# Splitting the stored rows into seven batches and the last, and starting the expert layer inside the last batch's attention

## The reference

```python
def reference(x, ctx, mask, ...):
    x = x + mamba_block(layernorm(x))            # own layernorm, conv, scan in chunks, gated norm, residual
    x = x + cross_attention(layernorm(x), ctx, ctx, adj, mask, Wq, bq, Wk, bk, Wv, bv, Wo, bo)
    x = x + expert_layer(layernorm(x))
    return x

def expert_layer(x):                             # x: batch, position, feature
    scores = positional_encoding(512, 32) @ sign(tile_sigs).T
    expert = argmax(scores, axis=-1)             # one of 8 for each of the 512 positions, the same in all batches
    return W[expert] @ x + b[expert]
```

## Time and profile before

| | us |
|---|---|
| median of 3 runs | 1262.71 |
| lowest, highest | 1261.99, 1266.43 |
| the profiled execution | 1266.53 |
| its span, first to last instruction | 1264.7 |
| granted TensorE clock, mean over the span | 0.969 of full speed |
| TensorE busy over the span | 1135.1 (90%) |
| DVE, ACT, POOL busy | 1005.2, 781.2, 634.1 |

### The profile page before, as it was taken

One profiled execution on the slowest core, in us unless ns is written; L12 is line 12 of the kernel. 1 busy time (PEld: TensorE's weight loads), 2 busy tenths in 40 slices (PEclk: granted clock), 3 DMA queues, 4 the chain that ended last, 5 costly groups with the idle time before them and its releaser, 6 DMA issues. The chain is left out here.

```text
span 1264.7 us, 29914 instructions
## 1 busy us (share of the span) xinstructions
PE 1135.1 (90%) x10292; PEld 840.7 (66%) x10292; DVE 1005.2 (79%) x2535; ACT 781.2 (62%) x1452; POOL 634.1 (50%) x554
## 2 busy tenths in 40 slices
PE   4687999999999999999999999999999999877397
PEld 2355677777777676867777777777776777755244
DVE  6866888888879887888888887888888877754486
ACT  2224676667666676667766766676566776766242
POOL 4572466337732684357544763278245753300475
PEclk9798999999999999999999999999899999989699
DMA  6042105400522024301440054104230133110511
GB/s 207 0 117 76 51 7 141 122 26 26 145 74 76 27 76 108 111 5 59 114 139 5 26 151 112 33 26 120 65 117 10 61 77 103 28 49 15 208 80 57
DMA packets 101524, 96.52 MB, mean 76 GB/s; under 512 B 17184, under 2 KB 76832, under 8 KB 100096
## 3 DMA queue, kind: packets, MB, share of 16 engines
q1 hardware_dynamic: 92912, 76.42, 20.4%
q0 software_dynamic: 6240, 17.57, 5.9%
q10 hardware_dynamic: 2224, 0.62, 0.2%
HBM read 71.49 MB, written 27.26 MB: 78 GB/s over the span
## 5 line engine op out<-in xcount | busy, mean ns | idle before, releaser
L907 ACT ACTIVATE T<-T,nmx 128x512 f32<-128x512 f32 x512 | 369.2, 724 | 214.7 <-DVE nmx L1278 211.8
L1278 DVE CUSTOM_DVE_ANT_0 T<-ps,am 128x512 f32<-128x512 f32 x512 | 348.0, 685 | 108.8 <-PE ps L501 106.6
L697 PE MATMUL pt<-ident,T 128*128 128x128 f32 x2048 | 314.1, 276 | 15.5 <-ACT PT L898 14.1
L697 PEld LDWEIGHTS pt<-ident,T 128*128 128x128 f32 x2048 | 250.0, 142 | 93.6 <-issue 42.3
L501 PE MATMUL ps<-k_st,q_st 128*128 128x512 f32 x512 | 261.5, 512 | 24.8 <-DMA q_st<-q_d 24.8
L898 ACT COPY PT<-pt 128x512 f32<-128x512 f32 x352 | 201.7, 573 | 16.4 <-PE pt L697 16.2
L1394 POOL TENSOR_TENSOR dmask<-triu,dA 128x1024 fp32r<-128x1024 f32 x64 | 132.7, 2137 | 49.5 <-DVE dA L1122 49.4
L716 PE MATMUL po<-PT,va 128*17 128x128 f32 x4096 | 137.6, 275 | 13.4 <-issue 7.0
L501 PEld LDWEIGHTS ps<-k_st,q_st 128*128 128x128 f32 x512 | 98.9, 193 | 55.1 <-DMA q_st<-q_d 28.0
L716 PEld LDWEIGHTS po<-PT,va 128*17 128x17 f32 x4096 | 102.4, 97 | 36.8 <-issue 35.4
L1369 POOL TENSOR_TENSOR xc<-xc,ygT 128x512 f32<-128x512 f32 x90 | 119.9, 1332 | 13.4
(11 more groups left out here) (218 smaller groups left out, 1968.3 us busy)
## 6 DMA issues: line engine op xcount, KB each, us to landing
k_st<-k_d SPq DMA_DIRECT2D x256, 64.0 KB, 2.2
q_st<-q_d SPq DMA_DIRECT2D x256, 64.0 KB, 2.4
am<-in_mask SPq DMA_DIRECT2D x8, 1024.0 KB, 5.4
k_d<-kp SPq DMA_DIRECT2D x32, 256.0 KB, 2.6
am<-in_adj POOLq DMA_DIRECT2D x8, 1024.0 KB, 10.8
q_d<-qp SPq DMA_DIRECT2D x128, 64.0 KB, 1.6
xio<-in_x SPq DMA_DIRECT2D x8, 512.0 KB, 4.3
xio<-in_ctxT SPq DMA_DIRECT2D x8, 512.0 KB, 4.1
```

What stands on the lines that cost most here:

```text
L697: ins = pe.transpose(pt[u % 2][:, kt * P:(kt + 1) * P], T[:, u % RING, kt * P:(kt + 1) * P], ident[:, :])
L907: act.activation(T[:, u % RING, :], T[:, u % RING, :], ACT.Exp, bias=nmx[:, u % RING:u % RING + 1], scale=-1.0).then_inc(sems["probs"], 1)
L1278: dve.tensor_tensor_reduce(T[:, u % RING, :], ps[(a * UNITS + u) % S_BANKS][:, :], ams[a % 2][:, qt, :], -1.0, 3e38, ALU.add, ALU.min, nmx ...
```

## The change

The tensor x2_d becomes two: x2_early holds the rows of batches 0 to 6 (7 KB a position), x2_late those of batch 7 (1 KB). Each block is gathered twice, from the one and from the other. New stages of the last batch only put expert work into its attention: "fb" the gathers of the biases, "fg" those of blocks 0 to 3 from x2_early (both on POOL), "fw" the load of the expert weights (SP), "fs" the statistics of blocks 0 to 2 for seven batches, two rows a slot in twelve consecutive slots (DVE), "fr" their powers (POOL), "fl" the placing of the weights of blocks 0 and 1 (ACT, eight copies). For that the tiles are laid out anew: the weights lie over wxbc, wz and pre (one tile proj), the biases over xt, xdt and xw (x3), the placed weights over am_0, am_1, th with sq and zs (tsz), and T, and the six blocks' rows have a buffer each.

The pairs are put in another order (PAIR): first the three pairs of batches 0 to 5 of blocks 0 to 3, twelve in all, then the pairs of batches 6 and 7 of these blocks, then blocks 4 and 5. They start within the slots: pair i stands in slot F_AT + 3 i on TensorE, a slot earlier on DVE (normalise) and a slot later on ACT (copy_pair), for the first five; the rest follow in loops. In a slot the pair stands behind the stages, so pair 0 follows the last group of weighted sums. POOL, in its loop of pairs, issues the gathers of blocks 4 and 5 at pairs 3 and 4, the six late gathers at pairs 6 to 8, the powers of the remaining groups of rows after pairs 3, 10, 14 and 18, and the scatters at pairs 14 to 17 and 21 and at the end. The third and fourth tiles' "ot" and "op" of the last batch get places of their own (FINAL).

```diff
+LAST = B - 1
+AHEAD = 4
+PAIR = [(k, n) for k in range(AHEAD) for n in range(B // 2 - 1)] + [(k, B // 2 - 1) for k in range(AHEAD)] + [(k, n) for k in range(AHEAD, BLOCKS) for n in range(B // 2)]
+ROWS = [[(k, j) for j in range(B - 1)] for k in range(AHEAD)] + [[(k, B - 1) for k in range(AHEAD)]] + [[(k, j) for j in range(B)] for k in range(AHEAD, BLOCKS)]
+SUMMED = [max(i for i, (kk, n) in enumerate(PAIR) if kk == k) + 1 for k in range(BLOCKS)]
+STATS_IN = 3
+PLACED_IN = 2
+PLACE_AT = (0, 4, 14, 16)
+STATS_AT = [(g, (2 * n, 2 * n + 1)) for g in range(STATS_IN, AHEAD) for n in range(B // 2)] + [(None, None)] * 6 + [(AHEAD, range(AHEAD))] + [
+    (g, (2 * n, 2 * n + 1)) for g in range(AHEAD + 1, BLOCKS + 1) for n in range(B // 2)]
...
+STAGES.update({("fw",): {"sp": 880}, ("fb",): {"pool": 600}})
+STAGES.update({("fg", k): {"pool": tick} for k, tick in enumerate((700, 820, 740, 780))})
+STAGES.update({("fs", k, n): {"dve": 980 + 80 * k + 20 * n} for k in range(STATS_IN) for n in range(B // 2)})
+STAGES.update({("fr", k): {"pool": 1045 + 80 * k} for k in range(STATS_IN)})
+STAGES.update({("fl", k, j): {"act": (1000, 1120)[k] + 20 * j} for k in range(PLACED_IN) for j in range(P // SEG)})
+FINAL = {
+    ("ot", 2): {"pe": 1080, "act": 1100}, ("op", 2): {"pe": 1140, "dve": 1150, "sp": 1160},
+    ("ot", 3): {"pe": 1400, "act": 1400}, ("op", 3): {"pe": 1420, "dve": 1420, "sp": 1440},
+}
...
+F_AT = SLOTS - 13
+F_PACE = 3
+def pairs_at(s_, ahead):
+    i, r = divmod(s_ - F_AT + ahead, F_PACE)
+    return [i] * (r == 0 and 0 <= i < PAIRS)
...
-        x2_d = nc.dram_tensor("x2_d", (S, ROW), F32, kind="Internal").ap()
+        x2_early = nc.dram_tensor("x2_early", (S, LAST * E), F32, kind="Internal").ap()
+        x2_late = nc.dram_tensor("x2_late", (S, E), F32, kind="Internal").ap()
...
+                    if k == "fw":
+                        last = latest([("bc", i) for i in range(CT)] + [("z", c) for c in range(C)], b)
+                        sp.wait_ge(full(last, b), full_at(last, b))
...
+                        sp.dma_start(w_f, t["w_f"].rearrange("(k p) t e -> p k t e", p=P)).then_inc(step["f_w"], 16)
...
+                def pair(i):
+                    pe.wait_ge(step["f_normed"], 2 * (i + 1))
+                    pe.wait_ge(step["f_copied"], max(0, i - 1))
+                    if i < 2:
+                        pe.wait_ge(sems[evac_by(UNITS - 2 + i)], at(evac_by(UNITS - 2 + i), LAST, evac_at(UNITS - 2 + i)))
...
+                    ins.then_inc(step["f_turned"], 1)
+                    if i:
+                        product(i - 1)
+                def product(i):
+                    pe.wait_ge(step["f_placed"], P // SEG * (PAIR[i][0] + 1))
+                    pe.wait_ge(step["f_copied"], i + 1)
+                    pe.wait_ge(step["f_sum"], max(0, i - 1))
...
+                def copy_pair(i):
+                    act.wait_ge(step["f_turned"], i + 1)
+                    act.wait_ge(step["f_product"], max(0, i - 1))
+                    act.copy(t_f[:, i % 2, :], pt[i % 2][:, :]).then_inc(step["f_copied"], 1)
+                    for k in range(PLACED_IN, BLOCKS):
+                        for j in range(P // SEG):
+                            if i == PLACE_AT[k - PLACED_IN] + j // (1 + (k == AHEAD)):
+                                place(k, j)
...
+                def normalise(i):
+                    k, n = PAIR[i]
+                    dve.wait_ge(step["f_rstd"], rows_of(i) + 1)
+                    dve.wait_ge(step["f_turned"], max(0, i - 1))
...
+                    if g is not None:
+                        stats(g, part)
+                    if i >= 2:
+                        add_product(i - 2)
...
+                for i in range(PAIRS):
+                    if i == 3:
+                        pool.wait_ge(sems["pv"], at("pv", B, 0))
+                    if 3 <= i < 3 + BLOCKS - AHEAD:
+                        early(AHEAD + i - 3)
+                    if i == 6:
+                        pool.wait_ge(step["f_x2_late"], 16 * C)
+                    if 6 <= i < 6 + BLOCKS // 2:
+                        late(2 * (i - 6))
+                        late(2 * (i - 6) + 1)
+                    bias(i)
+                    if i < len(STATS_AT) and STATS_AT[i][0] is not None and len(ROWS[STATS_AT[i][0]]) - 1 in STATS_AT[i][1]:
+                        rstd(STATS_AT[i][0])
+                    for k in range(BLOCKS):
+                        if SUMMED[k] + 1 == i:
+                            scatter(k)
                 scatter(BLOCKS - 1)
```

More of the change, by code:

```diff
@@ L170, in schedule @@
                     where = FIRST.get(stage, where)
+                if b == LAST:
+                    where = FINAL.get(stage, where)
                 if stage[0] == "conv":
@@ L490, in _ @@
                         m(stg, b)
[L492 to L495 removed]
+                sp.wait_ge(step["f_out"], 16 * BLOCKS)
             @block.tensor
@@ L1254, in conv, with add_product @@
+                def add_product(i):
+                    k, n = PAIR[i]
+                    dve.wait_ge(step["f_biased"], i + 1)
+                    dve.wait_ge(step["f_product"], i + 1)
+                    two = x_f[k][:, 2 * n * E:2 * (n + 1) * E]
+                    dve.tensor_tensor(two, ps[i % 2][:, :], two, ALU.add).then_inc(step["f_sum"], 1)
                 def conv(b, mt):
@@ L1346, in _ @@
+                for i in pairs_left(1):
+                    normalise(i)
+                for i in (PAIRS - 2, PAIRS - 1):
+                    add_product(i)
             @block.gpsimd
@@ L1475, in _, with late @@
[L1475 to L1490 removed]
+                def late(k):
+                    pool.indirect_dma_start(x_f[k][:, LAST * E:ROW], None, x2_late, bass.IndirectOffsetOnAxis(row_of[:, k:k + 1].bitcast(U32), 0),
+                                            bounds_check=S - 1, oob_is_err=False).then_inc(f_in_late[k], 16)
@@ new lines, in bias, with scatter @@
+                def bias(i):
+                    k, n = PAIR[i]
+                    pool.wait_ge(step["f_normed"], 2 * (i + 1))
+                    rows = x_f[k][:, 2 * n * E:2 * (n + 1) * E].rearrange("p (b e) -> p b e", e=E)
+                    pool.tensor_tensor(rows, rows, b_f[:, k, :].rearrange("p (o e) -> p o e", o=1).broadcast_to([P, 2, E]), ALU.add).then_inc(step["f_biased"], 1)
+                def scatter(k):
+                    pool.wait_ge(step["f_sum"], SUMMED[k])
+                    pool.indirect_dma_start(t["out"], bass.IndirectOffsetOnAxis(row_of[:, k:k + 1].bitcast(U32), 0), x_f[k], None,
+                                            bounds_check=S - 1, oob_is_err=False).then_inc(step["f_out"], 16)
```

255 lines of the change are left out of this document (136 added, 119 removed).

## The result

The changed kernel takes 1254.38 us (median of 4 runs, 1252.68 to 1255.53) against 1263.20 for the kernel before (4 runs): a ratio of 0.992, 95% interval 0.9895 to 0.9945, so 6.9 to 13.3 us less. The forecast was 1246. The direction came out as predicted and the time lies inside the range; the gain, 8.8 us by the medians, is about half of the 16.5 of the forecast.

A forecast was written before the change was run, and what follows sets the result against it. TensorE was taken as the limit within blocks of pairs, with a hole at the end; 27.0 us saved less 10.5 of new costs left 16.5, so 1262.71 - 16.5 = 1246 us, range 1238 to 1257.

The forecast's parts named there:

- signs of being wrong: Listed signs: sums waiting for bias adds, indirect DMAs over 1.2 us, later row maxima, TensorE waiting over 7 us for queries.
- Query loads: Third tile's query write and read in the last attention, delayed by the row gathers: 1.0 us, from -0.7 to 3.
- Statistics and weights: Last sixteen heads: DVE's statistics add 5.0 us, ACT's weight copies nothing, waiting for the expert weights 0.5.
- The copies: ACT's eight placings of expert weights in the last attention, 5.0 us of work in idle time: nothing, at worst 5.0.
- the third projection: Third tile's output projection, moved between the last scores where TensorE idles 4.6 us: costed at nothing.
- Start of the pairs: After the last group of weighted sums, the transposes of pair 3 start 10.4 us later.
- POOL among the pairs: Pairs 3 to 21: POOL's 51.7 us against TensorE's 44.1 and 4.1 slack, plus stretched normalisations: 4.0 us, 0 to 8.
- End: What follows the transposes of pair 23 stays as before: 9.33 us.
- The carry to the median: Profiled execution 1266.53 us, median of runs 1262.71; the 16.5 us gain was taken over to the median unchanged.
- POOL sets the pace: Rival: POOL limits the expert pairs with no slack used, costing 8 to 12 us, so 1250 to 1254; chance 0.14.
- The attention takes the added work in full: Rival: no added work in the last attention hides in idle time; 25.8 us in all, no change, 1261.5; chance 0.10.
- The lock falls on POOL: Rival: DVE halts POOL's work among the pairs, stretched by 2.1; 1303 us, slower; chance 0.04.

The follow-up runs named there:

- e3: The changed kernel with the statistics in the last batch's attention reading 8 of 256 features per row, output off; 1253.95 us, ratio 0.991.
- e4: The changed kernel with POOL's bias additions touching 8 of 256 features of each batch, other biases left out; 1251.44 us, ratio 0.9895.
- e5: e1 with the load of the expert weights issued earlier, behind the third tile's query read; 1246.00 us, ratio 0.9854.
- e1: The changed kernel with the four early row gathers held until the third tile's queries have landed; 1245.71 us, ratio 0.9845.
- e6: e5 with the statistics of blocks 0 to 2 reading 8 of 256 features, output off; 1242.73 us, ratio 0.9828.
- e9: e6 with ACT's eight copies of expert weights in the attention moving 8 of 256 features, output off; 1242.46 us, ratio 0.9821.
- e12: e6 with the third tile's output projection moved back behind the last scores, ahead of pair 0, output off; 1246.03 us, ratio 0.9867.
- e10: e8 with POOL's gathers and scatters reordered away from pairs with powers, and blocks 0 to 2's statistics in other places; 1241.85 us, ratio 0.9822.
- e2: The changed kernel with the four early gathers fetching 1 KB rows of input x instead of 7 KB rows, output meaningless; 1247.29 us, ratio 0.9877.
- e8: e5 with e7's spread gathers and block 0's statistics ahead of the fourth tile's first head; 1243.08 us, ratio 0.9831.
- e7: e1 with POOL's indirect gathers spread one to a pair over pairs 3 to 10; 1248.68 us, ratio 0.9865.
- e11: e8's statistics with e10's order of POOL's work, nothing left out; 1238.19 us, ratio 0.9805.

## Why the prediction was right, and where it was too high

From W to the end the prediction's sum says 160.57 - 27.0 + 10.5 = 144.07; it took 149.11. The 5.0 us between them, term by term (one of its own signs of being wrong came true: TensorE waiting over 7 us for the third tile's queries; it waited 10.21):

- **Query loads: the mis-sized term, 3.6 of the 5.0.** Taken at 1.0 with 3 as the upper bound. From W to S4 it went from 38.50 (10.98 + 27.52) to 43.06 (16.58 + 26.48), 4.56 more; the third tile alone lost 5.60, and in e3 and e4, with the same gathers, W to S4 was 44.56 and 45.08. The mechanism was named nearly right (a write that waits until the gathers have drained; it shared the engines with them, packet by packet, and ended with them); two choices failed. The drain was put near 1112, for at most 3.7 MB at the 430 GB/s of the earlier trace rows, gathers with nothing beside them; it was 3.1 MB, but here the engines moved 287 and then 326 GB/s, and the last gather, issued at 1107.03, landed 9.4 us later, at 1116.4, with the read issued at 1115.61. And between a write that waits for the drain (3) and one that is faster (-0.7) the middle was taken, where the trace shows the full delay: 11.02 against 5.49, 5.5 us.
- **Statistics and weights: right as a sum, in part by luck.** 5.0 + 0 + 0.5 = 5.5 forecast, 5.32 measured (31.66 - 26.34). DVE was nearly full in the twelve slots, as forecast (21.99 us of the 24.17 from 1147.65 to the third power's start). The 0.5 for the weights was meant as the length of the wait; the wait was 2.58 and cost 0.5 only because the statistics hid the rest. (A step is 0.88 by the prediction's own row, so its 10.4 should be 10.6; that is nothing here.) Of it 0.5 are the weights (e5 against e1), 3.1 the features that the statistics read (e6 against e5, of which 0.3 to 0.4 may be the clock, which fell in e5 alone), the rest probably the steps as such. The copies cost 0 (e9), the third projection 0 between the scores (e12).
- **Start of the pairs: right.** 10.4 forecast, 10.0 measured, in every kernel that kept the projection early.
- **POOL among the pairs: the right engine, 1.6 low, and near by luck.** 4.0 forecast (0 to 8), 54.62 - 49.02 = 5.6 measured. Of the 4.0, 3.5 were for POOL's 51.7 us as a whole against the pitches and the slack; there was no such shortage: POOL was busy 44.47 of 54.62, and e10 does nearly the same work (43.17) at a cost of 0.2. The loss comes from single pairs at which two pieces of work stand ahead of an addition, which the lock turns into a halted normalisation, or a halted addition to the variances, longer than DVE's idle time. The prediction had this collision as well, at one addition each (1.54 us) in "some four pairs" and within the pitch. Eight normalisations took over a microsecond, four of them 2.01 to 3.16.
- **End:** 9.77 against 9.33, the remaining 0.4.
- **The carry to the median.** The profiled execution of before took 1266.53, more than any of its four runs (median 1263.20), and the sum was made against it. From W to the end the change wins 11.5, by the medians 8.8. Of the difference of 2.6, 0.46 lies ahead of W (1104.13 against 1104.59); the rest is that the profiled execution of before was 3.33 over its median and that of the changed kernel 1.15 over its own, and where those lie no trace tells. Both gains are within the interval of 6.9 to 13.3.

**The rivals.** *POOL sets the pace* named the right engine, and its 1250 to 1254 lies nearer to the measured 1254.38 than the forecast of 1246, but by luck: it rests on 8 to 12 us for POOL, which cost 5.6, and on a limit that was not there, as e10 does POOL's work in 49.23. *The attention takes the added work in full* is refuted by e9, where 2.8 us less of ACT's work save nothing, by the 2.58 us of waiting that were worth 0.5, and by the stretch itself, which grew by 5.32 where that rival has 18.8 (10.4 + 5.0 + 3.4). *The lock falls on POOL* is refuted by rows of every kernel: the indirect DMAs took 0.98 to 1.21 us and the whole bias additions 1.26 to 1.32. Between additions and DVE the loser was DVE each time. The Trainium skill's figure in SBUF — State Buffer, "A bandwidth-pool intuition that's wrong", 3.1 us for a DMA from GpSimd's queue beside a copy on DVE, did not appear in any of these runs; the normalisations beside them were short, 0.4 us an instruction, so beside a long one it stays open.

That large rows delay another queue's write has a sentence of the Trainium skill beside it: DMA: Bandwidth & Descriptors, "SWDGE vs HWDGE vs iDMA", says that a DMA engine takes its queues in turn. By that one might expect a write of 0.26 MB to be through well ahead of the end of 3.1 MB of gathers. The trace agrees with the turns, 348 packets against 337 in the 5 us shown above, and shows why the write was late all the same: a turn was a packet, 7 KB for the one and 512 bytes for the other.

## What to carry to other kernels

A large transfer that is moved "out of the way" goes somewhere: look at which small write on the same DMA engines has a reader waiting, and hold the large one until that reader has its data, if its own reader comes late. Count the small write in packets, not in bytes, when large packets share the engines with it. Where one engine halts another, look at how long each halt is against the idle time it falls into, and not at busy time: nearly the same POOL work cost 5.6 us in one order and 0.2 in another. And where two waits lie over each other (weights and statistics here), removing either one alone tells little; the experiment is to remove both.

## What the runs showed of the hardware

The granted clock. TensorE idled 2.63 us ahead of the fourth tile's first score in the changed kernel, and then ran at 0.50, the level of 1.2 GHz, through the next heads:

```profile
1149.03:1151.20 2.17, 1.87 (x9) 1.39 (x7) 2.15 (x8) 2.17 (x4) 0.00 (x0) 0.50 1.01 423
```

In the first 4.30 us of the same heads e9 had a mean of 0.61 and e6, which differs only in ACT's copies and had idled 2.75 us, kept the full clock:

```profile
1138.08:1142.38 4.30, 4.09 (x18) 3.33 (x19) 2.92 (x11) 2.91 (x5) 0.00 (x0) 0.61 0.00 0
```

```profile
1138.11:1142.41 4.30, 3.19 (x20) 2.38 (x20) 3.29 (x15) 2.92 (x6) 0.00 (x0) 1.00 0.00 0
```

Within some 1.2 us of the fourth tile's first score the clock fell in the changed kernel, e1, e2, e5, e8 and e9, and not in the others; the idle time ahead was 2.44 to 3.07 us where it fell and 1.92 to 2.97 where it did not. In e3, e4 and e7 it fell some 9 us behind that score, while TensorE idled 2.31 to 2.76 us behind ACT's wait for the weights, in e10 12 and in e11 19 us behind it, where the idle times were shorter (1.47 us in e10). Over these sixteen heads it stayed full only in e6, e12 and the kernel before. What decides it stays open. It cost little: by the fifth row maximum e9 was 0.3 to 0.4 us behind e6, and it did not fall further behind.
